# Four elementwise jobs moved from VectorE to ScalarE, and the two halves of a step's scores set side by side on TensorE

## What is computed

```python
xn = layernorm(x)                                   # [16, 512, 128]
# block 1
h = layernorm(xn) * g1 + b1
q, k, v = heads(h@WQ+bQ), heads(h@WK+bK), heads(h@WV+bV)   # 16 heads of 8
attn = softmax(where(window of 128 keys, q k^T / sqrt(8), -inf)) @ v
ssm = scan(s = A*s + h@Bw) @ Cw
gate = sigmoid(h@Wg + bg)
x1 = xn + gate*(attn@WO + bO) + (1-gate)*ssm
s = x1 + gelu(layernorm2(x1)@W1 + b1)@W2 + b2
# block 2
xc = bf16(xn); normed = bf16(xc * rsqrt(mean(xc^2)+eps) * norm_weight)
combine = softmax of the 2 largest of 8 logits (normed@gate_weight^T + bias)
out2 = xc + sum_e combine_e * expert_e(normed)
result = x + s * silu(out2)
```

## Time and profile before

| | |
|---|---|
| median of 3 runs | 1066.67 us (1065.89 to 1070.92) |
| the profiled execution's own time | 1065.71 us |
| its span | 1063.9 us |
| mean granted TensorE clock | 0.976 of 2.4 GHz |
| busy TensorE / VectorE / ScalarE / GpSimd | 84% / 74% / 66% / 47% of the span |
| one pass with all its work | about 60.2 us |

### The profile page before, as it was taken

How to read it: one execution, slowest core, us unless ns; L and a number is a source line. 1 busy time by engine, 2 the same in 40 slices (tenths; PEclk the granted TensorE clock), 3 DMA queues, 4 the chain that set the end, 5 groups by cost and what they waited for, 6 DMA issues and landing times.

```text
span 1063.9 us, 38011 instructions
## 1 busy us (share of the span) xinstructions
PE 892.8 (84%) x15736; PEld 541.7 (51%) x15736; DVE 783.0 (74%) x2015; ACT 696.9 (66%) x1094; POOL 501.0 (47%) x786
## 2 busy tenths in 40 slices
PE   2476898989889898988889898888989898888887
PEld 1333564645555464645556464555646364554535
DVE  4466777888777778798777678777778878866415
ACT  3205585857668595857768485776858686765755
POOL 6225446373636446273635527353554727243331
PEclk9999999999999999999999899999999999989959
DMA  5651414224241504223241322424150332410000
GB/s 104 139 120 63 102 41 110 39 92 64 84 87 47 123 19 119 52 92 64 78 95 47 88 53 92 64 77 94 47 114 18 105 55 94 64 37 6 26 1 11
DMA packets 85597, 75.22 MB, mean 71 GB/s; under 512 B 9329, under 2 KB 79154, under 8 KB 85426
## 3 DMA queue, kind: packets, MB, share of 16 engines
q1 hardware_dynamic: 83346, 72.00, 28.7%
q10 hardware_dynamic: 2080, 0.79, 0.3%
HBM read 36.33 MB, written 30.15 MB: 62 GB/s over the span
## 4 chain that ended last, share of the span: by engine, by line
PE 47%; DVE 26%; issue 14%; ACT 9%; POOL 2%; DMA 2%; DVEq 0%; SPq 0%; POOLq 0%; ACTq 0%
PE ps L502 6%; PE ps L692 5%; PE ps L560 5%; DVE mx L1080 5%; PE ps L752 5%; PE ps L713 5%; ACT pt L833 4%; PE ps L491 3%; DVE nf L960 3%; PE ps L577 3%; DVE gc L1139 3%; DVE lin L1132 2%; PE ps L686 2%; PE ps L517 2%; DVE junk L952 2%
## 5 line engine op out<-in xcount | busy, mean ns | idle before, releaser
L833 ACT ACTIVATE pt<-ps 128x1024 f32<-128x1024 f32 (+1 forms) x256 | 234.4, 916 | 201.4 <-PE ps L491 199.9
L1080 DVE TENSOR_REDUCE mx<-ps 128x2 f32<-128x320 f32 (+1 forms) x512 | 231.0, 466 | 88.5 <-PE ps L517 85.8
L1261 POOL TENSOR_SCALAR_AFFINE_SELECT pt<-pt 128x512 f32<-128x512 f32 x256 | 170.6, 668 | 241.2 <-ACT pt L833 240.6
L502 PE MATMUL ps<-kd,qz 48*32 48x160 bf16 (+1 forms) x4096 | 157.8, 239 | 82.9 <-DVE mx L1080 49.9
L502 PEld LDWEIGHTS ps<-kd,qz 48*32 48x32 bf16 x4096 | 73.3, 90 | 229.6 <-issue 113.9
L491 PE MATMUL ps<-qz,kd 51*32 51x256 bf16 (+1 forms) x4096 | 180.1, 269 | 7.6 <-ACT pt L833 4.2
L560 PE MATMUL ps<-pt,va 128*32 128x256 f32 (+1 forms) x2048 | 156.7, 380 | 11.8 <-ACT ot L838 6.3
L692 PEld LDWEIGHTS ps<-m,act_t 128*128 128x128 f32 x1024 | 126.8, 191 | 53.6 <-DVE act_t L1160 38.6
L692 PE MATMUL ps<-m,act_t 128*128 128x128 f32 x1024 | 143.2, 283 | 11.6 <-DVE act_t L1160 11.6
L1264 POOL TENSOR_SCALAR_AFFINE_SELECT pt<-pt 128x512 f32<-128x512 f32 x192 | 124.5, 648 | 0.0
L881 ACT ACTIVATE lin<-ps,mbias 128x512 f32<-128x512 f32 x128 | 87.6, 684 | 48.7 <-DVE act_t L1160 29.4
(11 more groups left out here) (158 smaller groups left out, 1611.8 us busy)
## 6 DMA issues: line engine op xcount, KB each, us to landing
qz<-qk_parts SPq DMA_DIRECT2D x32, 384.0 KB, 7.0
kd<-qk_parts SPq DMA_DIRECT2D x32, 384.0 KB, 8.8
qk_parts<-qp SPq DMA_DIRECT2D x16, 384.0 KB, 2.4
qk_parts<-kp SPq DMA_DIRECT2D x16, 384.0 KB, 2.3
xl<-L_attn_x SPq DMA_DIRECT2D x16, 256.0 KB, 3.2
qk_parts<-qp SPq DMA_DIRECT2D x16, 256.0 KB, 2.9
qk_parts<-kp SPq DMA_DIRECT2D x16, 256.0 KB, 2.7
xnr<-xn SPq DMA_DIRECT2D x16, 256.0 KB, 3.3
```

Source lines behind the costliest of these rows:

```text
L502: nc.tensor.matmul(ps[QG * c:QG * (c + 1), 4 + par, w * pr:w * (pr + 1)], qz[q][rows, 2 * g + pr, P * i + QG * c:P * i + QG * (c + 1)], kd ...
L833: nc.scalar.activation(to, src, ACT.Exp, scale=SCALE).then_inc(exp_ok.sem, 1)
L1080: nc.vector.tensor_reduce(mx[:, i, HG * g + pr:HG * (g + 1):2], src, AX.X, ALU.max).then_inc(mx_ok.sem, 1)
L1261: sel1 = nc.gpsimd.affine_select(out=pt[:, s, :, 0:P], in_=pt[:, s, :, 0:P], compare_op=ALU.is_ge, fill=0.0, base=0, pattern=[[0, HG], [1, ...
```

## The change

- **Squares.** ScalarE takes the square of `xc` with a running sum, one instruction for each 128 x 128 tile (steps 6 and 7). They stand ahead of the copy of k in step 6.
- **Input scaling.** ScalarE scales `xc` by the root, four instructions, in steps 10 and 11; `nf` becomes float32. The factor norm_weight is applied after the transpose, as a scale for each partition in the ScalarE copy `nfn`. The four transposes of `nf` are now of float32 instead of bfloat16.
- **Value rows and gate.** The biases bV and bg come in as a matmul of ones with a split of the bias into three bfloat16 parts, 512 columns wide, that starts the accumulation in bank 3. One ScalarE copy then writes the values, one ScalarE tanh reads the gate from PSUM in step 12. `gpre` and the tanh at the start of the pass are gone; `gth` has three buffers. The layout of `va` is new (each pair of heads side by side, 41 wide), so WV and bV are permuted once at the start, and each buffer row is 28% longer.
- **TensorE's order.** The halves of the scores of step n now follow each other, and the values of step n-3 come behind both.
- **VectorE's order.** The second part of `finish` goes from half step 3 to 4, the scan from 18 to 19, the pieces of `route_mix` from 9, 11, 15, 16 to 6, 7, 12, 15.
- At the start VectorE permutes WV and bV and splits the biases: 11 small instructions.

```diff
-MIX = (9, 11, 15, 16)
+MIX = (6, 7, 12, 15)
...
-        nf = sb("nf", [P, NT, D], BF16)
+        nf = sb("nf", [P, NT, D])
...
-        va = sb("va", [P, 3, NT, H, VW])
+        va = sb("va", [P, 3, NT, H // 2, 2, VW + OV])
...
+                def add_bias(n):
+                    nc.tensor.matmul(bank_t(3), onesb[0:65], bias3[0:65, n].unsqueeze(1).to_broadcast([65, NT, P]), start=True, stop=False, skip_group_check=True)
+
                 def project_v():
                     pe.wait_ge(*done(st_ok, b + 2))
+                    if start(b, -2):
+                        pe.wait_ge(bias_set.sem, 9)
+                    add_bias(0)
                     for t in range(NT):
-                        mm = nc.tensor.matmul(bank_t(3)[:, t], hT[:, P * t:P * (t + 1)], wv[:], start=True, stop=True)
+                        mm = nc.tensor.matmul(bank_t(3)[:, t], hT[:, P * t:P * (t + 1)], wv[:], start=False, stop=True, skip_group_check=True)
...
                 for n in range(NCH + 4):
                     if n < NCH:
                         scores(b, q, n, 0)
+                        scores(b, q, n, 1)
                     if main and 3 <= n < NCH + 3:
                         values(b, q, n - 3)
-                    if n < NCH:
-                        scores(b, q, n, 1)
...
-                if nxt:
-
-                    act.wait_ge(*done(gpre_ok, b + 1))
-                    act.wait_ge(*done(x1_ok, b - 1))
-                    nc.scalar.activation(gth[:, 1 - q], gpre[:], ACT.Tanh, scale=0.5).then_inc(gth_ok.sem, 1)
-
...
+                def v_in():
+                    act.wait_ge(*done(v_ps, b + 2))
+                    act.wait_ge(*done(pv_ps, b - 1))
+                    nc.scalar.activation(va[:, (b + 2) % 3].rearrange("p t g k v -> p t (g k) v")[:, :, :, 0:DH],
+                                         bank_t(3).rearrange("p t (h v) -> p t h v", v=DH), ACT.Copy).then_inc(v_ok.sem, 1)
+
+                def gate_in():
+                    act.wait_ge(*done(g_ps, b + 2))
+                    act.wait_ge(*done(x1_ok, b - 1))
+                    nc.scalar.activation(gth[:, (b + 2) % 3], bank_t(3), ACT.Tanh, scale=0.5).then_inc(gth_ok.sem, 1)
+
+                def square(t):
+                    act.wait_ge(*done(xc_ok, b + 2))
+                    act.wait_ge(*done(rs_step, b + 1))
+                    act.wait_ge(*done(nfT_ps, b + 1))
+                    nc.scalar.activation(nf[:, t], xc[:, q, t], ACT.Square, accum_out=sq[:, t:t + 1]).then_inc(sq_ok.sem, 1)
+
+                def norm_f(t):
+                    act.wait_ge(*done(rs_step, b + 2))
+                    act.wait_ge(*done(sq_ok, b + 2))
+                    nc.scalar.activation(nf[:, t], xc[:, q, t], ACT.Copy, scale=rs[:, t:t + 1]).then_inc(nf_ok.sem, 1)
...
+                        if n in (AT_SQ, AT_SQ + 1):
+                            square(2 * (n - AT_SQ))
+                            square(2 * (n - AT_SQ) + 1)
+                        if n in (AT_NF, AT_NF + 1):
+                            norm_f(2 * (n - AT_NF))
+                            norm_f(2 * (n - AT_NF) + 1)
+                        if n == AT_V:
+                            v_in()
+                        if n == AT_G:
+                            gate_in()
...
-                    nc.scalar.activation(nfn[:], bank_bf(6), ACT.Copy).then_inc(nfn_ok.sem, 1)
+                    nc.scalar.activation(nfn[:], bank(6), ACT.Copy, scale=cols["nw"][:]).then_inc(nfn_ok.sem, 1)
...
-                        if has(b - 1) and step in (1, 3):
-                            finish(b - 1, step // 2)
+                        if has(b - 1) and step in (1, 4):
+                            finish(b - 1, step // 2 // 2)
...
-                            if step in (2 * AT_SQ, 2 * AT_SQ + 1):
-                                squares(b + 2, q, (0, 1) if step == 2 * AT_SQ else (2, 3))
...
-                            if step == 2 * AT_U + 2:
+                            if step == 2 * AT_U + 3:
                                 recur()
-                            if step in (2 * AT_NF, 2 * AT_NF + 1):
-                                norm_f(b + 2, q, (0, 1) if step == 2 * AT_NF else (2, 3))
-                            if step == 2 * AT_V + 2:
-                                v_in()
-                            if step == 2 * AT_G + 2:
-                                gate_in()
```

More of the change, by code:

```diff
@@ L122, in build @@
         w2 = sb("w2", [P, NJ, P])
-        cols = {n: sb(n, [P, 1]) for n in ("ln1_g", "ln1_b", "bQ", "bK", "ln2_g", "ln2_b")}
+        cols = {n: sb(n, [P, 1]) for n in ("ln1_g", "ln1_b", "bQ", "bK", "ln2_g", "ln2_b", "nw")}
         b1c = sb("b1c", [P, NJ])
         acol = sb("acol", [P, 1])
-        rows = {n: sb("row_" + n, [P, P]) for n in ("bV", "bg", "b2", "nw")}
+        rows = {n: sb("row_" + n, [P, P]) for n in ("bV", "bg", "b2")}
         gbias_b = sb("gbias_b", [P, E], BF16)
@@ L370, in build @@
         ]
-        ONES = [(st[N:N + 1], 1.0), *((va[:, i, :, HG * g:HG * (g + 1), OV * (g % 2) + DH:OV * (g % 2) + OV], 1.0) for i in range(3) for g in range(NG))]
+        ONES = [(st[N:N + 1], 1.0), *((va[:, i, :, :, :, DH:OV], 1.0) for i in range(3))]
         ALL_BLANKS = len(BLANKS) + len(LATER_BLANKS)
@@ L607, in project_g @@
                     pe.wait_ge(*done(v_ok, b + 2))
+                    add_bias(1)
                     for t in range(NT):
-                        mm = nc.tensor.matmul(bank_t(3)[:, t], hT[:, P * t:P * (t + 1)], wg[:], start=True, stop=True)
+                        mm = nc.tensor.matmul(bank_t(3)[:, t], hT[:, P * t:P * (t + 1)], wg[:], start=False, stop=True, skip_group_check=True)
                     mm.then_inc(g_ps.sem, 1)
@@ L1008, in _, with values_setup @@
                 nc.vector.memset(dst, value).then_inc(blank_set.sem, 1)
+            def values_setup():
+                dve.wait_ge(weights_in.sem, 16 * len(WEIGHTS))
+                for dst, src in ((wv, ob[:, 0]), (rows["bV"], ob[:, 1])):
+                    nc.vector.tensor_copy(dst[:].rearrange("p (s c k v) -> p s c k v", s=NS, c=HG, k=2), paired(src)).then_inc(values_set.sem, 1)
+                dve.wait_ge(values_set.sem, 2)
             def later_setup():
@@ L1020, in later_setup, with bias_setup @@
                 all_set(dve)
+            def bias_setup():
+                dve.wait_ge(weights_in.sem, 16 * len(WEIGHTS))
+                dve.wait_ge(blank_set.sem, len(BLANKS))
+                for n, name in enumerate(("bV", "bg")):
+                    nc.vector.tensor_copy(nfn[:, P * n:P * (n + 1)], rows[name][:]).then_inc(bias_set.sem, 1)
+                dve.wait_ge(bias_set.sem, 2)
+                for n, name in enumerate(("bV", "bg")):
+                    nc.vector.tensor_tensor(ob[:, 2 + n], rows[name][:], nfn[:, P * n:P * (n + 1)], ALU.subtract).then_inc(bias_set.sem, 1)
+                nc.vector.tensor_copy(bias3[0:1], nfn[0:1, 0:2 * P].rearrange("p (n d) -> p n d", n=2)).then_inc(bias_set.sem, 1)
+                dve.wait_ge(bias_set.sem, 5)
+                nc.vector.tensor_copy(nfn[:, 0:2 * P].rearrange("p (n d) -> p n d", n=2), ob[:, 2:4]).then_inc(bias_set.sem, 1)
+                dve.wait_ge(bias_set.sem, 6)
+                nc.vector.tensor_copy(bias3[32:33], nfn[32:33, 0:2 * P].rearrange("p (n d) -> p n d", n=2)).then_inc(bias_set.sem, 1)
+                nc.vector.tensor_tensor(ob[:, 2:4], ob[:, 2:4], nfn[:, 0:2 * P].rearrange("p (n d) -> p n d", n=2), ALU.subtract).then_inc(bias_set.sem, 1)
+                dve.wait_ge(bias_set.sem, 8)
+                nc.vector.tensor_copy(bias3[64:65], ob[64:65, 2:4]).then_inc(bias_set.sem, 1)
             def body(b, q):
@@ L1065, in body @@
                 if start(b, -2):
+                    values_setup()
+                    bias_setup()
                     later_setup()
```

62 lines of the change are left out of this document (19 added, 43 removed).

## The result

The changed kernel took 1052.22 us (median of 4 runs, 1050.54 to 1053.38) against 1068.44 (4 runs, 1065.89 to 1070.92): a ratio of 0.984, with a 95% interval of 0.981 to 0.987. The forecast was 1045 in a range of 1030 to 1066. The profiled execution took 1053.38 us, its span 1051.6, 12.3 less than the 1063.9 of before.

The account below looks back on a forecast made before the run. It saw TensorE busiest overall, waiting 3.1 us a score stage for the maxima of VectorE, the fullest engine there. Terms of -1.6 us times 14 passes (-22.5) and +0.7 for edges took 1065.7 to 1043.9, so 1045 as median, range 1030 to 1066.

Parts of the forecast that it names:

- The six terms: Score stage, exponentials 6 to 13: changes of +0.2, -0.55, -0.13, -0.2, -1.25 and +0.12 us a pass.
- the -0.13 of step 8 to 9: Step bound by TensorE alone: 2.18 against 2.31 us, from the adjacent score halves alone.
- The square: ScalarE's square with a sum, steps 6 and 7: priced at 0.40 us each, between 0.31 and 0.73.
- only change places with the maxima: nothing: Steps 2 to 4: moving finish and the first pieces of route_mix on VectorE was to cost nothing.
- the tanh that leaves the end of a pass: End of the expert stage: given nothing since TensorE's states hold the next step; up to 0.5 if that cover is gone.
- the sum itself: All full passes: -1.6 us a pass times 14 passes gives -22.5 us.
- a granted clock below that of before: Listed among the signs that the forecast is wrong, for the clock after the change; no size given.
- VectorE's 11 setup instructions fall in its wait for `va`: Start of the kernel: the new setup on VectorE hides while GpSimd clears va, itself +1.45 us.
- VectorE's -97: Sign of being right: VectorE's busy time down by some 97 us, the four moved groups.
- ScalarE as the bound: Slower rival: additions of 4.0 us a pass paid in series between ScalarE's exponentials, +1.9 x 14 = 27, 1093 us; chance 13%.
- The gain is given back: Rival: late copies of q and k and a square at 0.73 undo 1.45 of 1.6 us a pass, 1063 us; 13%.
- Only TensorE is left: Rival: TensorE's waits for VectorE and ot vanish except about 1.0 in steps 1 and 2; 2.6 a pass, 1030 us; 8%.

Follow-up runs that it names:

- e1: The kernel before with only TensorE's new order (both score halves, then the values): 1074.2 us, ratio 1.002 to 1.008 to the kernel before.
- e5: The changed kernel with VectorE's old places for the routing pieces, finish and the scan: 1061.4 us, ratio 0.989 to 0.997 to the kernel before.
- e3: The changed kernel with squares and input scalings back on VectorE and bfloat16 nf: 1054.2 us, ratio 0.982 to 0.991 to the kernel before.
- e2: The changed kernel with TensorE's old order, values between the score halves: 1059.7 us, ratio 0.987 to 0.995 to the kernel before.
- e6: The changed kernel with ScalarE's squares moved behind the copy of k: 1047.6 us, ratio 0.978 to 0.987 to the kernel before.
- e7: The changed kernel with q and k writes cut to one partition of 128 from the third batch element on: 1039.7 us, ratio 0.970 to 0.978.
- e8: The changed kernel with all of VectorE's extra jobs behind the second maximum of a step: 1020.7 us, ratio 0.952 to 0.960 to the kernel before.
- e10: The kernel before with TensorE's new order and VectorE's jobs behind the second maximum, none moved to ScalarE: 1032.8 us, ratio 0.961 to 0.971.

## Why the prediction was right, and where not

- **The place of the gain was right.** Step by step, before, forecast, after: 6 to 7 2.21, 2.4, 2.08; 7 to 8 2.37, 1.80, 1.89; 8 to 9 2.31, 2.18, 2.16; 9 to 10 1.73, 1.53, 1.54; 10 to 12 5.25, 4.0, 3.89; 12 to 13 2.34, 2.46, 2.33. The six terms gave -1.8 and measured -2.3. But the -0.13 of step 8 to 9 is not "from the adjacent halves alone": that step is 2.71 in e1 and in e5, and 2.16 only where VectorE's pieces have left their old places.
- **The square was mis-sized.** At 0.40 two of them were 0.8. They are 0.30 apart, the square (0.20 to the next instruction) and the reading of its sum (0.10): 0.6. The Trainium skill (ScalarE: Activation LUTs, What ACT_TABLE_LOAD costs) gave an estimate of 0.29 for the square; its row says 304 ns, so the trace agrees. Its rule to put adds and multiplies on VectorE (Rules for kernel authors) does not hold for this kernel: e3 puts squares and scalings there and its pass is 1.15 longer.
- **Two zeros were not zeros.** That `finish` and the first pieces of `route_mix` "only change places with the maxima: nothing" was wrong: exponential 0 to 6 takes 10.73, before 10.19 in most passes (10.38 in the pass of the earlier trace rows), while the forecast had +0.2 there. e5 shows 0.25 of it as `finish`. Another 0.28 lies in steps 0 to 2 (1.63 and 1.94, before 1.52 and 1.77); e1 has the old values and e3 and e5 the new, so it comes with the new form of the values and the gate, and why is open. For the tanh that leaves the end of a pass the forecast gave nothing, "up to 0.5" if its cover was gone: from exponential 15 to the next 0 it is 30.45 instead of 30.71.
- **The step that failed is the sum itself**, 14 passes times the gain of an undisturbed one. It took the falls of the clock and the pauses as equal before and after. They took back 16.8 of 26.6. The prediction named "a granted clock below that of before" only as a sign of error, with no price; in the 14 passes it was 0.979 against 0.992. The early falls go with the adjacent halves: six in e1 and in the change, none in before and in e2. But how many there are, the halves do not fix (none in e6, two in e7, one in e8, with the same order on TensorE), and each count is of one run. Why the change has more pauses than before is open.
- **That 1052 lies in the range is in part luck.** Three errors met: the gain of an undisturbed pass was 1.9 and not 1.6 (4 us better), the surplus 17 us worse, and the edges 3 us better (next point).
- **Edges.** "VectorE's 11 setup instructions fall in its wait for `va`" failed. `va` took 1.5 more, as forecast (5.22, now 6.73), but VectorE's last setup cast stuck behind it and the constants of `st` started at 22.88 instead of 21.00. The first exponential is 2.7 late, forecast 0.7 for both edges. The pass behind the full ones and the end, which the forecast had at nothing, were 5.0 shorter, so the edges gave 2.3 instead of costing 0.7.
- **VectorE's -97** was -56: small jobs of the mixing got longer in their new places (four of these groups by 24 us in all), and the setup is new. The cast to `cp` by line and shape, before and after:
```profile
L998 DVE CAST cp<-cr 128x32 bf16<-128x32 f32 x16 | 3.3, 205 | 0.0
```
```profile
L1020 DVE CAST cp<-cr 128x32 bf16<-128x32 f32 x16 | 12.5, 779 | 0.0
```
- **Rivals.** ScalarE as the bound did not come: exponential 11 does start right behind ScalarE's own copy, as the sum had it, but 2.49 after exponential 10 and not late, and exponential 12 waits for TensorE. "The gain is given back" came true by two thirds of the gain, but from another source than the late copies that it named. "Only TensorE is left" was 1030 since it took the waits in steps 1 and 2, about 1.0 a pass, as fixed; e8 removes 0.4 of that with an order of VectorE (step 1 to 2 is 1.54, in the change 1.94), and is at 1021. Three of the prediction's sums are a little off: 3.7 less 1.0 is 2.7 and not 2.6 a pass (1029); the gain less 1.45 leaves 1065 and not 1063; 1045 with 9 and 6 is 1060 and not 1058. None changes a case.

## What to carry to other kernels

Price a job on an in-order engine by what is queued behind it, not by its length alone. Put behind the last thing that the bound engine waits for in a step, the same jobs cost 1.7 us less of a pass, at 91% load (e1 and e10); they were still not free, since moving them away was worth another 1.6 (e8). Count the waits that a tighter order leaves bare as well as those it removes; the clock and the pauses of the bound engine belong in the sum, with a range of their own. Judge a change by its undisturbed pass and by its surplus apart, or a gain in the one hides a loss in the other.
